# A decoder layer on one core: wide activations transposed by DMA, block maxima folded for two batches together, third norm on ScalarE, keys placed by spread DMAs, engine orders rewritten

## The chip, the cores and the metric

One core of one Trainium2 chip. The metric is the device time of one execution in microseconds. The kernel before takes 292.42 us, the median of three runs (292.4 to 292.68).

## The reference

Sixteen sequences (batches) of 128 tokens with 256 features go through one decoder layer. A post-norm follows each of three parts; the last part has a norm of its own inside.

```python
def attn(x):                     # L0_attn: q, k, v projections, no softmax
    kvt = jnp.cumsum(k * v, axis=-2) * denom
    return jnp.einsum('bse,fe->bsf', q * kvt, Wo)
def xattn(q, k, v):              # 32 query heads, 8 key heads, head size 8, 128 context rows
    weights = jax.nn.softmax(qh @ kh / sqrt(8)); return weights @ vh
def ffn(inputs):                 # blocks of 32: shared power-of-two scale, 8-bit steps
    x = residual = bf16_round(inputs)
    h = mx_layernorm(x, ln_w, ln_b)
    h = mx_gelu(mx_linear(h, W1, b1))          # 256 -> 1024
    return bf16_round(residual + mx_linear(h, W2, b2))   # 1024 -> 256
x = layernorm(x + attn(x)); x = layernorm(x + xattn(x, ctx, ctx)); x = layernorm(x + ffn(x))
```

`mx_quant`, inside `mx_linear`, takes the largest magnitude of each block of 32, cuts it to its exponent, and rounds the block's values to steps of that power of two.

## The kernel before

The 16 batches go as 8 pairs (`PB` = 2 batches, `NP` = 8). Every engine has its own hand-ordered instruction stream: a `head` written out call by call, a `step(p, on)` that is unrolled four times (t = 5 to 8), and a `tail` written out again. In step t the list `p` holds the pairs t, t-1, ... t-6, so `p[1]` is in its projections, `p[2]` and `p[3]` in cross attention, `p[4]` in the feed-forward part and `p[5]`, `p[6]` in its end. Nothing but these orders and the semaphore waits sets when work runs. A loop step thus does the work of one pair.

What the change and the prediction's steps touch:

- Cross attention. `keys_rounded` (POOL, L536 on) splits the keys into `k3r`; `keys(p, b, u)` (POOL, L555) multiplies them with a mask into the one buffer `kbd`, four instructions a pair, so that the four key heads lie on a block diagonal. PE computes the scores twice: `scores_a` (L2122) for the maxima, which DVE takes with `maxima` (L1323, 16 a pair), and `scores_b` (L2156) with the maximum subtracted, which ACT exponentiates (`exps`, L857). The maxima travel through a PE transpose (`maxT`), an ACT copy (L845) and, for the pairs 1 to 6, a small DMA issued by SP (`max_rows`, L397) into the rows of `xT`. `keys(p, ...)` waits for the last `scores_b` of the pair before, since `kbd` is single.
- The third norm. DVE's `moments` and `mean_var` of `xb_all` give mean and variance; POOL's `var_eps` (L504) and `rstd` (L509) the factor; DVE's `norm3` (L1361, two a pair) applies it; POOL's `weight3` (L593) and `shift3` (L599) apply weight and shift; DVE's `quantise_h` (seven steps: L1411, 1414, 1416, 1418, 1420, 1422, 1424) quantises both batches together.
- The wide activations `g_sb` (128 x 1024 a batch, after the gelu). `quantise_g(p, b, i)` on DVE has ten steps a batch: magnitude (L1465), two foldings by halves (L1467, 512 and 256 columns), a reduction to 32 block maxima (L1470), three steps on 32 columns (L1414, 1416, 1418), and three over 1024 columns (L1420, 1422, 1424). Then PE transposes the result (`g_T`, L2222, eight matmuls a batch), ACT copies it into `gT` (`gT_copy`, L881), and PE multiplies (`ffn_down`, L2233 and L2235).
- The end of a pair. ACT's `y2_copy` (L912), POOL's `ffn_out` (L605) and `residual3` (L612), DVE's moments, the norm on ACT (`norm4`, L903), and the store by SP.
- Weights. In the head DVE quantises both weight matrices between the other work (L1242 to L1271).
- `warm`, `warm_p` and `warm_last` on PE (L2001, L2013, L2007) are matmuls of zeros whose results nobody reads.

## Time and profile before

| what | value |
| --- | --- |
| median of the runs | 292.42 us |
| time of the profiled execution | 291.33 us |
| its span, first to last instruction | 289.6 us |
| mean granted TensorE clock | 0.988 |
| PE busy | 270.8 us (94%), 1640 matmuls |
| DVE busy | 261.2 us (90%), 682 instructions |
| ACT busy | 220.2 us (76%), 378 instructions |
| POOL busy | 174.1 us (60%), 253 instructions |
| DMA | 12.68 MB, mean 44 GB/s |

Spans of PE, DVE and ACT overlap with the next instruction's, so that a row's mean duration is longer than what the instruction takes from its engine; the distance from start to start, where nothing is waited for, is what it takes. The chain that ended last runs 44% on PE, 37% on DVE, 6% on ACT and 3% on POOL.

### The profile page before, as it was taken

How to read it: one execution, taken by the hardware profiler on the slowest of the kernel's cores; microseconds unless marked ns; L12 is line 12 of the kernel's file. 1: busy time of each engine (PE TensorE's matmuls, PEld its weight loads, DVE VectorE, ACT ScalarE, POOL GpSimd, SP SyncE). 2: the span in 40 equal slices, each digit the busy share in tenths (PEclk: the TensorE clock that was granted, in tenths of full speed). 3: DMA queues.
4: the chain of work that ended last, by engine and by line, in shares of the span. 5: the costliest groups of instructions: out<-in, count | busy, mean ns of one | idle time of the engine just before them, and what ended most of it. 6: DMA issues, size and time to landing. Idle time of an engine off the chain costs nothing.

```text
span 289.6 us, 5338 instructions
## 1 busy us (share of the span) xinstructions
PE 270.8 (94%) x1640; PEld 165.4 (57%) x1640; DVE 261.2 (90%) x682; ACT 220.2 (76%) x378; POOL 174.1 (60%) x253
## 2 busy tenths in 40 slices
PE   8999998999997998999989998999699989997799
PEld 3776755477554764676566756575346444543454
DVE  3799999996999999999999999999986997799982
ACT  5131866479999699979998889889998899875650
POOL 2746380698466787868786878667777353533321
PEclk9999999999999999999999999999869999999999
DMA  7931200002110020022002200210010000100111
GB/s 239 381 125 36 65 3 0 9 6 71 37 43 0 8 71 15 1 67 77 16 1 63 79 9 5 66 44 9 7 36 5 3 0 0 37 3 1 37 38 38
DMA packets 11053, 12.68 MB, mean 44 GB/s; under 512 B 3216, under 2 KB 8336, under 8 KB 10768
## 3 DMA queue, kind: packets, MB, share of 16 engines
q1 hardware_dynamic: 10592, 11.55, 12.5%
q10 hardware_dynamic: 432, 0.79, 0.7%
q8 instruction: 13, 0.21, 0.3%
q14 instruction: 16, 0.13, 0.2%
HBM read 9.84 MB, written 2.10 MB: 41 GB/s over the span
## 4 chain that ended last, share of the span: by engine, by line
PE 44%; DVE 37%; issue 8%; ACT 6%; POOL 3%; DMA 1%; DVEq 0%; POOLq 0%
DVE nm L1323 9%; PE bank L2122 6%; PE bank L2156 6%; PE bank L2169 5%; DVE st L1278 4%; PE bank L2007 3%; PE bank L2235 3%; PE bank L2210 3%; PE bank L2056 2%; PE bank L2082 2%; DVE gq L1424 2%; PE bank L2069 2%; PE bank L2208 2%; ACT g_sb L877 1%; PE bank L2177 1%
## 5 line engine op out<-in xcount | busy, mean ns | idle before, releaser
L1323 DVE TENSOR_REDUCE nm<-bank 128x4 f32<-128x512 f32 x128 | 83.8, 677 | 0.8 <-PE bank L2122 0.6
L857 ACT ACTIVATE p_sb<-bank 128x512 f32<-128x512 f32 x128 | 72.3, 599 | 12.1 <-PE bank L2156 11.6
L2122 PE MATMUL bank<-kbd,xT 96*128 96x512 f32 x128 | 56.0, 468 | 2.6 <-ACT xT L828 1.5
L2156 PE MATMUL bank<-xT,kbd 104*128 104x512 f32 x128 | 53.0, 444 | 5.3 <-DMA xT<-mT 3.2
L555 POOL TENSOR_TENSOR kbd<-k3r,diag_sb 96x512 fp32r<-96x512 f32 x32 | 33.2, 1052 | 12.9 <-PE bank L2156 12.9
L2156 PEld LDWEIGHTS bank<-xT,kbd 104*128 104x128 f32 x128 | 24.6, 193 | 18.6 <-ACT p_sb L857 6.4
L2122 PEld LDWEIGHTS bank<-kbd,xT 96*128 96x128 f32 x128 | 24.4, 193 | 17.9 <-DVE nm L1323 10.8
L2169 PE MATMUL bank<-p_sb,va_sb 128*32 128x512 f32 x256 | 33.3, 610 | 0.0
L509 POOL TENSOR_TENSOR rs<-ve,nhalf 128x2 f32<-128x2 f32 (+1 forms) x36 | 26.1, 725 | 4.6
L504 POOL TENSOR_SCALAR ve<-mv 128x2 f32<-128x2 f32 (+1 forms) x36 | 8.4, 234 | 33.5 <-DVE mv L1284 31.8
L2043 PE MATMUL bank<-wkv_r,xt_r 128*128 128x512 f32 x84 | 23.8, 405 | 0.7 <-DVE r_sb L1301 0.7
L871 ACT ACTIVATE y_sb<-bank 128x512 bf16<-128x512 f32 x32 | 19.1, 596 | 5.5 <-PE bank L2210 4.8
L828 ACT ACTIVATE xT<-bank 96x512 fp32r<-96x512 f32 x32 | 18.6, 586 | 5.5 <-PE bank L2106 5.4
L1278 DVE BATCH_NORM_STATS2 st<-r_sb 128x6 f32<-128x256 f32 x48 | 19.3, 416 | 0.6 <-POOL r_sb L612 0.3
L2106 PEld LDWEIGHTS bank<-idr,x 128*96 128x96 f32 x128 | 14.2, 164 | 9.5 <-issue 3.6
L2210 PE MATMUL bank<-w1T,hT 128*128 128x512 bf16 x64 | 19.1, 379 | 0.0
L2007 PE MATMUL bank<-zero_b 128*128 128x512 bf16 x80 | 18.9, 379 | 0.0
L881 ACT ACTIVATE gT<-bank 128x1024 bf16<-128x1024 bf16 x16 | 16.4, 1022 | 2.9 <-PE bank L2222 2.8
L605 POOL TENSOR_TENSOR s_sb<-y_sb,xb_all 128x512 bf16<-128x512 bf16 x7 | 8.3, 1185 | 16.7 <-ACT y_sb L912 16.7
L2043 PEld LDWEIGHTS bank<-wkv_r,xt_r 128*128 128x128 f32 x84 | 15.6, 189 | 4.5 <-issue 1.3
L2106 PE MATMUL bank<-idr,x 128*96 128x128 f32 x128 | 17.6, 261 | 0.5 <-ACT xT L850 0.5
L877 ACT ACTIVATE g_sb<-y_sb 128x1024 bf16<-128x1024 bf16 x16 | 16.9, 1057 | 0.4
(133 smaller groups left out, 619.1 us busy)
## 6 DMA issues: line engine op xcount, KB each, us to landing
xt_sb<-in_xt SPq DMA_DIRECT2D x8, 256.0 KB, 2.9
x_sb<-in_x SPq DMA_DIRECT2D x8, 256.0 KB, 2.9
out_dram<-o_sb SPq DMA_DIRECT2D x7, 256.0 KB, 2.2
k_sb<-in_ctx SPq DMA_DIRECT2D x8, 192.0 KB, 3.0
x_all<-in_w SPq DMA_DIRECT2D x1, 1024.0 KB, 6.2
w_raw<-in_w SPq DMA_DIRECT2D x1, 1024.0 KB, 8.3
p_sb<-in_wkv ACTq DMA_DIRECT2D x2, 256.0 KB, 3.9
cv_sb<-in_ctxv SPq DMA_DIRECT2D x8, 64.0 KB, 2.0
```

The costliest lines, as they stand in the source:

```text
L509: gp.tensor_tensor(rs[:, part(b)], ve[:, part(b)], nhalf[:, part(b)], ALU.pow).then_inc(rs_ready, batches(b))
L555: gp.tensor_tensor(kbd[0:MR, b, u, :, :], k3r[:, b, u, :].bitcast(F32).unsqueeze(1).to_broadcast([MR, KU, P]), diag_sb[0:MR, :].unsqueeze( ...
L857: sc.activation(p_sb[:, k, :], bankB[k % 2][:, :], ACT.Exp, scale=SCORE_SCALE).then_inc(s_ex, 1)
L1278: ve.bn_stats(st[:, b, :], rows).then_inc(st_ready, 1)
L1323: ve.tensor_reduce(nm[:, b, u, g, :], bankA[(2 + k + 11 * b) % 2][:, :].rearrange("p (k t) -> p k t", k=KU), AX.X, ALU.max, negate=True).t ...
L2007: mm(bankB[0][:, :], zero_b[:, 0:P], zero_b[:, :], start=True, stop=True)
L2043: last = mm(bankP[b][:, :], xt_r[:, a, c, b, :], wkv_r[:, w, c, :], start=c == 0 and n == 0, stop=c == KC - 1 and n == len(PARTS) - 1)
L2106: last = mm(bk[0:MR, g * P:(g + 1) * P], x3[:, b, u, g, :, :].rearrange("p a r -> p (a r)"), idr[:, :], start=True, stop=True)
L2122: mm(bankA[(2 + k + 11 * b) % 2][:, :], xT[0:MR, b, u, g, :], kbd[0:MR, b, u, :, :].rearrange("r k t -> r (k t)"), start=True, stop=True). ...
L2156: mm(bankB[k % 2][:, :], kbd[0:MR + 2 * KU, b, u, kk, :], xT[0:MR + 2 * KU, b, u, :, :].rearrange("r g s -> r (g s)"), start=True, stop=Tr ...
L2169: last = mm(value_bank(p, b)[VW * k:VW * (k + 1), :], va_sb[:, at0:at0 + VW], p_sb[:, u * KU + k, :], start=u == 0, stop=u == U - 1, tile_ ...
L2210: last = mm(bk[:, :], hT[:, c, b, :], w1T[:, c, cols], start=False, stop=c == KC - 1)
```

## The change

- `g_T` and `gT_copy` go for the pairs 0 to 4 (`BY_DMA` = 5). SP issues one transposing DMA a batch, `gT[:, b] <- gq[:, b, :]`, after the last step of `quantise_g`. `ffn_down` waits for its landing. Pairs 5 to 7 keep PE's transposes.
- `quantise_g` has six steps a batch (magnitude, foldings to 512 and 256, and the three over 1024 columns). Between them six new steps `g_scales(p, i)` work on both batches in one instruction each: foldings to 128, 64 and 32 columns a batch in place of the two reductions, and the three small steps, now on bf16 maxima. The last pair has twelve steps a batch (`last_quantise_g`) with the same foldings.
- `norm3` moves from DVE to ACT for the pairs 0 to 6 (`pair_norm3`); POOL computes its shift (`shift_product`, `shift` with `nb3`, two more small instructions a pair).
- `keys` goes from POOL for the pairs 1 to 7: SP copies the four heads by four DMAs a pair into `kbd[p % 2]`, now two buffers. Pair 0 keeps the POOL multiplications, one DMA copies the mask rows to the second buffer, and POOL zeroes it once.
- `last_x2` goes from DVE to ACT (`norm2_x2(7, b)`, behind the last gelu).
- Every head, step and tail has a new order, with other places and numbers of the `warm` matmuls.

The core of the diff:

```diff
+            def keys(p, k):
+                if k == 0:
+                    sp.wait_ge(s_k3r, 2 * p + 2)
+                    if p == 1:
+                        sp.wait_ge(s_seta, 5)
+                    else:
+                        sp.wait_ge(s_sbm, 16 * (p - 1))
+                sp.dma_start(kbd[p % 2][k:MR:KU, :, :, k, :].bitcast(F32), k3r[k:MR:KU, :, :, :].bitcast(F32)).then_inc(s_kbd, 16)
+
+            def transpose_g(p, b):
+                sp.wait_ge(s_q2[b], GSTEPS * (p + 1))
+                if later(p):
+                    sp.wait_ge(s_f2, upto(p - 1, b))
+                sp.dma_start_transpose(gT[:, b, :, :], gq[:, b, :]).then_inc(s_gTd[b], 16)
...
             def step(p, on):                         # SP
+                if on[1]:
+                    load_x(p[1])
                 if on[3]:
                     max_rows(p[3], 1)
                 if on[0]:
                     load_xt(p[0])
+                if on[2]:
+                    max_rows(p[2], 0)
                 if on[1]:
-                    load_x(p[1])
-                    load_values(p[1])
-                if on[2]:
-                    max_rows(p[2], 0)
+                    keys(p[1], 0)
+                if on[4]:
+                    transpose_g(p[4], 0)
+                if on[1]:
+                    keys(p[1], 1)
                 if on[5]:
                     store(p[5])
+                if on[1]:
+                    keys(p[1], 2)
+                    load_values(p[1])
+                    keys(p[1], 3)
+                if on[4]:
+                    transpose_g(p[4], 1)
                 if on[0]:
                     load_keys(p[0])
...
             def step(p, on):                         # POOL, from its middle
                 if on[4]:
                     var_eps(p[4], mv3, ve3, s_mv3, s_ve3)
                     rstd(p[4], ve3, rs3, s_ve3, s_rs3)
+                    shift_product(p[4], mv3, rs3, nb3, s_rs3, s_nb3)
+                    shift(p[4], nb3, s_nb3)
+                if on[2]:
+                    split_x1_high(p[2], 1)
+                if on[4]:
                     weight3(p[4])
                     shift3(p[4])
-                if on[2]:
-                    keys(p[2], 0, 0)
-                    keys(p[2], 0, 1)
+                if on[0]:
+                    split_xt_high(p[0])
                 if on[5]:
                     ffn_out(p[5])
                     residual3(p[5])
...
+            def pair_norm3(p, b):                    # ACT
+                act.wait_ge(s_nb3, 2 * p + 2)
+                sc.activation(h0_sb[:, b, :], batch_of(xb_all, p, b), ACT.Identity, bias=nb3[:, 1, b:b + 1],
+                              scale=rs3[:, b:b + 1]).then_inc(s_h0, 1)
...
+            def fold_g(batches, i):                  # DVE
+                if i == 0:
+                    return ve.tensor_scalar(gz2[:, batches, :].bitcast(U16), g_sb[:, batches, :].bitcast(U16),
+                                            MAGNITUDE, None, ALU.bitwise_and)
+                into = am2 if i == FOLDS - 1 else gz2
+                n = F >> i
+                return ve.tensor_tensor(into[:, batches, 0:n], gz2[:, batches, 0:n], gz2[:, batches, n:2 * n], ALU.max)
+            def g_scales(p, i):
+                if i == 0:
+                    for b in range(PB):
+                        dve.wait_ge(s_q2[b], GSTEPS * p + BATCH_FOLDS)
+                else:
+                    dve.wait_ge(s_gs, SSTEPS * p + i)
+                both = slice(0, PB)
+                folds = FOLDS - BATCH_FOLDS
+                last = fold_g(both, BATCH_FOLDS + i) if i < folds else scale_step(both, i - folds)
+                last.then_inc(s_gs, 1)
...
             def step(p, on):                         # DVE, its end
                 if on[4]:
+                    g_scales(p[4], 0)
                 if on[3]:
                     mean_var(p[3], 1, st2, mv2, s_st2, s_mv2)
                 if on[4]:
+                    g_scales(p[4], 1)
+                    g_scales(p[4], 2)
+                    g_scales(p[4], 3)
+                    g_scales(p[4], 4)
+                    g_scales(p[4], 5)
                 if on[0]:
                     k_times_v(p[0], 0)
+                if on[4]:
+                    quantise_g(p[4], 0, 3)
+                    quantise_g(p[4], 1, 3)
+                    quantise_g(p[4], 0, 4)
+                    quantise_g(p[4], 0, 5)
```

In the new DVE step `quantise_h(p[4], 0)` comes behind `maxima(p[2], 0, 0)`; before it came ahead of it. The new DVE step begins with `maxima(p[3], 1, 1)`, `quantise_g(p[5], 1, 4)`, `maxima(p[3], 1, 2)`, `quantise_g(p[5], 1, 5)`. In the new ACT step the two `pair_norm3` stand directly behind `q_copy`. In the new PE step `ffn_down(p[5], 0)` and `(p[5], 1)` keep their places behind `maxT(p[3], 1)` and `x1T(p[2], 0, 1)`, and `q_proj(p[1], 1)` stands eight calls earlier.

## Rows read from the trace of the kernel before

**Rows 1.** Busy time by stretch: start:end, length, then each engine's busy us (instructions)
```profile
20.00:40.00 20.00, 19.44 (x110) 13.71 (x110) 19.89 (x44) 9.64 (x18) 12.90 (x20) 1.00 0.12 37
```
**Rows 2.** The same view for one whole loop step
```profile
118.71:148.33 29.62, 28.72 (x182) 18.47 (x180) 28.54 (x76) 26.81 (x49) 22.64 (x32) 1.00 0.13 39
```
**Rows 3.** Groups by line and shape, 60 to 210 us: busy, mean ns, idle before
```profile
L1323 DVE TENSOR_REDUCE nm<-bank 128x4 f32<-128x512 f32 x82 | 53.5, 676 | 0.5 <-PE bank L2122 0.4
```
**Rows 4.** DVE timeline, end of a loop step: start, us, instruction
```profile
117.37 0.59 DVE L1470 TENSOR_REDUCE am<-gz 128x32 f32<-128x256 bf16 x1
117.87 0.17 DVE L1284 BATCH_NORM_AGGREGATE mv<-st 128x2 f32<-128x6 f32 x1
...
118.42 0.17 DVE L1416 TENSOR_SCALAR sc<-am 128x32 bf16<-128x32 f32 x1
...
118.71 0.69 DVE L1424 TENSOR_TENSOR gq<-gz,sc 128x1024 bf16<-128x1024 bf16 x1
```
**Rows 5.** DVE timeline, middle of the same step
```profile
125.64 0.73 DVE L1361 TENSOR_SCALAR h_sb<-xb_all,mv,rs 128x256 f32<-128x256 bf16 x2
126.29 1.28 DVE L1323 TENSOR_REDUCE nm<-bank 128x4 f32<-128x512 f32 x2
...
129.32 0.69 DVE L1411 TENSOR_REDUCE am<-h_sb 128x16 f32<-128x512 bf16 x1 [0.55 <-POOL h_sb L599]
...
130.35 0.96 DVE L1416 TENSOR_SCALAR sc<-am 128x16 bf16<-128x16 f32 x1
...
132.83 0.95 DVE L1424 TENSOR_TENSOR hq<-z,sc 128x512 bf16<-128x512 bf16 x1
```
**Rows 6.** POOL timeline beside rows 5
```profile
129.25 2.04 POOL L555 TENSOR_TENSOR kbd<-k3r,diag_sb 96x512 fp32r<-96x512 f32 x2
132.34 1.16 POOL L605 TENSOR_TENSOR s_sb<-y_sb,xb_all 128x512 bf16<-128x512 bf16 x1 [1.05 <-ACT y_sb L912]
```
**Rows 7.** Timelines of the head: DVE, then POOL
```profile
40.39 2.42 DVE L1268 TENSOR_SCALAR wqb<-wz 128x512 bf16<-128x512 int16 x1
...
44.85 0.49 DVE L1268 TENSOR_SCALAR wqb<-wz 128x512 bf16<-128x512 int16 x2
...
40.63 2.03 POOL L555 TENSOR_TENSOR kbd<-k3r,diag_sb 96x512 fp32r<-96x512 f32 x2
```
**Rows 8.** ACT timeline, middle of the same step
```profile
126.44 1.02 ACT L881 ACTIVATE gT<-bank 128x1024 bf16<-128x1024 bf16 x1
127.36 0.59 ACT L837 ACTIVATE q_sb<-bank 128x512 f32<-128x512 f32 x1
```
**Rows 9.** PE timeline, middle of the same step
```profile
128.54 0.27 PE L2233 MATMUL bank<-bias_h,ones_b 96*128 96x256 bf16 x1
...
130.36 0.28 PE L2233 MATMUL bank<-bias_h,ones_b 96*128 96x256 bf16 x1
```
**Rows 10.** DMA issues: count, KB each, median us to landing; then SP's timeline
```profile
xt_sb<-in_xt SPq DMA_DIRECT2D x8, 256.0 KB, 2.9
...
w_raw<-in_w SPq DMA_DIRECT2D x1, 1024.0 KB, 8.3
...
129.04 0.63 SPq L397 DMA_DIRECT2D xT<-mT  x1
```
**Rows 11.** Tail: DVE timeline, then PE timeline
```profile
219.24 0.69 DVE L1411 TENSOR_REDUCE am<-h_sb 128x16 f32<-128x512 bf16 x1 [2.87 <-POOL h_sb L599]
...
220.27 0.17 DVE L1416 TENSOR_SCALAR sc<-am 128x16 bf16<-128x16 f32 x1
220.47 0.17 DVE L1418 TENSOR_SCALAR in<-sc 128x16 int16<-128x16 int16 x1
...
221.54 0.42 DVE L1424 TENSOR_TENSOR hq<-z,sc 128x512 bf16<-128x512 bf16 x1
...
279.42 0.69 DVE L1424 TENSOR_TENSOR gq<-gz,sc 128x1024 bf16<-128x1024 bf16 x1
...
280.81 0.61 PE L2222 MATMUL bank<-idb,gq 128*128 128x128 bf16 x8
```

More of the change, by code:

```diff
@@ L33 @@
 EXPONENT = 0x7F800000
+EXPONENT16 = 0x7F80
 TINY = 2.0 ** -110
@@ L122, in decoder_kernel @@
         k3r = sb("k3r", [MR, PB, U, P], F32R)
-        kbd = sb("kbd", [P, PB, U, KU, P], F32R)
+        kbd = [sb(f"kbd{n}", [P, PB, U, KU, P], F32R) for n in range(2)]
         cv_sb = sb("cv_sb", [P, PB, KV, DH], F32)
@@ L272, in decoder_kernel @@
         s_nb2 = sem("shift2")
+        s_nb3 = sem("shift3")
         s_nb4 = sem("shift4")
@@ L290, in decoder_kernel @@
         s_q2 = [sem(f"g_quantised{b}") for b in range(PB)]
+        s_gs = sem("g_scales")
+        s_gTd = [sem(f"gT_landed{b}") for b in range(PB)]
         s_gTp = sem("g_transposed")
@@ L414, in head @@
                 load_x(0)
+                load_weight("w2")
+                load_keys(1)
+                load_xt(2)
+                load_x(1)
                 load_bias()
-                load_weight("ln")
-                load_weight("w2")
-                load_values(1)
-                load_x(1)
-                load_xt(2)
-                load_keys(1)
-                load_keys(2)
-                load_x(2)
-                load_xt(3)
+                load_xt(3)
+                load_keys(2)
+                keys(1, 0)
+                keys(1, 1)
+                load_x(2)
+                keys(1, 2)
+                keys(1, 3)
+                keys(2, 0)
+                second_diagonal()
+                load_values(1)
+                load_weight("ln")
+                max_rows(1, 0)
+                keys(2, 1)
+                keys(2, 2)
+                load_xt(4)
+                keys(2, 3)
+                max_rows(1, 1)
+                spread_bias()
                 load_values(2)
-                max_rows(1, 0)
-                max_rows(1, 1)
                 load_x(3)
                 load_keys(3)
-                spread_bias()
-                load_xt(4)
                 max_rows(2, 0)
+                keys(3, 0)
+                transpose_g(0, 0)
+                keys(3, 1)
+                load_keys(4)
+                keys(3, 2)
+                keys(3, 3)
                 load_values(3)
-                load_keys(4)
+                transpose_g(0, 1)
             def step(p, on):
+                if on[1]:
+                    load_x(p[1])
                 if on[3]:
@@ L980, in head @@
                 pv_copy(1, 0)
                 weights(2)
-                x1T(2, 0, 1)
+                q_copy(3)
                 exps(1, 1, 0)
+                weights(3)
                 exps(1, 1, 1)
-                weights(3)
                 exps(1, 1, 2)
+                hT_copy(0)
                 exps(1, 1, 3)
-                hT_copy(0)
                 exps(1, 1, 4)
+                hidden(0, 0, 0)
+                norm2_x2(0, 0)
                 exps(1, 1, 5)
-                hidden(0, 0, 0)
@@ L1694, in step @@
                     q_times_sum(p[1])
+                if on[2]:
+                    maxima(p[2], 0, 0)
                 if on[4]:
@@ L1813, in tail @@
                 quantise_h(5, 3)
+                maxima(7, 0, 0)
                 quantise_h(5, 4)
@@ L2392, in head @@
+                scores_a(2, 0, 0)
                 weights_T(2)
-                x1T(2, 0, 1)
+                scores_a(2, 0, 1)
+                running_sum(3)
+                scores_b(1, 1, 0)
+                weights_T(3)
+                scores_b(1, 1, 1)
+                values_back(1, 0)
+                scores_a(2, 0, 2)
+                scores_a(2, 0, 3)
+                scores_b(1, 1, 2)
+                h_T(0)
+                scores_b(1, 1, 3)
+                scores_a(2, 0, 4)
+                scores_b(1, 1, 4)
@@ L2431, in step @@
                 if on[3]:
+                    scores_a(p[3], 1, 0)
+                if on[1]:
+                    kv_proj(p[1], 0, 1)
+                if on[3]:
+                    x1T(p[3], 1, 1)
                     scores_b(p[3], 0, 0)
@@ L2474, in step @@
                     ffn_down(p[5], 0)
+                if on[2]:
+                    x1T(p[2], 0, 1)
+                    scores_a(p[2], 0, 0)
+                if on[5]:
+                    ffn_down(p[5], 1)
                 if on[3]:
@@ L2477, in step @@
                 if on[2]:
-                    x1T(p[2], 0, 1)
-                if on[5]:
-                    ffn_down(p[5], 1)
-                if on[2]:
-                    scores_a(p[2], 0, 0)
+                    scores_a(p[2], 0, 1)
                 if on[3]:
@@ L2554, in tail @@
                 weigh(6, 0, 0)
+                x1T(7, 0, 0)
                 maxT(6, 1)
-                g_T(4, 1)
-                x1T(7, 0, 0)
+                weigh(6, 0, 1)
+                scores_a(7, 0, 0)
                 x1T(7, 0, 1)
-                weigh(6, 0, 1)
+                warm_p(2)
                 ffn_down(4, 0)
+                scores_a(7, 0, 1)
                 scores_b(6, 1, 0)
```

1181 lines of the change are left out of this document (579 added, 602 removed).

## The prediction, as made before the run

> **What bounds the kernel now.** I read busy time by stretch first. In the head DVE is busy 19.89 of 20 us while ACT has 9.64 and POOL 12.90 [rows 1]. Then one whole loop step: 29.62 us, DVE 28.54, PE 28.72, ACT 26.81, POOL 22.64 [rows 2]. Two engines look full, so the groups decide: the 82 maxima that DVE takes between 60 and 210 us, each of which needs a fresh PE result, waited 0.5 us for PE in all [rows 3]. PE keeps ahead of DVE, its spans overlap, and its many short matmuls stretch when it has time. DVE is the bound from 20 us to about 210 us. There I count DVE time from start to start, and ask of each edit what it takes from DVE, and whether DVE will find its next input ready. The last 80 us are a chain from engine to engine in which DVE sometimes waits, as at 219.24 for POOL's h, 2.87 us [rows 11].
>
> **The change part by part.** The sum is made against the profiled execution (291.33 us, span 289.6); the median of the runs is 1.1 us above it, and I carry the difference over to the median.
>
> 1. *The third norm leaves DVE.* Two instructions, from 125.64 to the next start at 126.29: 0.65 us a pair [rows 5]. For the pairs 0 to 4 this lies where DVE is full: 5 x 0.65 = -3.25. For pairs 5 and 6 DVE waits for POOL anyway [rows 11], so nothing.
>
> 2. *Block maxima for two batches.* Out go, a pair, two reductions of 0.50 from start to start [rows 4] and six small steps, of which two took 0.29 from 118.42 to 118.71, 0.15 each: 1.0 + 0.9 = 1.9. In come six instructions that wait for one another. A dependent small step takes 0.20 from start to start (220.27 to 220.47) [rows 11]; three make 0.60, and the three foldings, which have 256, 128 and 64 results, lie between that 0.20 and the 0.50 of the reduction over 256 inputs: I take 0.35, 0.27 and 0.23. Together 1.45. That gains 0.45, but the new order also puts steps that wait for each other side by side (the last two over 1024 columns of batch 0, and the high and low part of the maxima), where the filler between them had hidden a delay of 0.1 to 0.2 each: about 0.35 back, and the gain that remains I take as 0. Bounds: -0.8 a pair if the foldings overlap with other work, +0.5 if they don't and each costs a reduction's 0.50.
>
> 3. *POOL in DVE's way.* The scale step of `quantise_h` on 16 columns took 0.96 us at 130.35, while POOL ran two `keys` from 129.25 to 131.29 [rows 5, 6]; without a neighbour the same step took 0.17 [rows 11]. This stands in four pairs (the scale step of the pairs 1 to 4, one in each of four loop-long periods), with 0.1 more on the step in front of it each time: 4 x 0.89 = -3.56. Behind it the last step of `quantise_h` took 0.95 beside POOL's `ffn_out` [rows 5, 6] against 0.42 alone [rows 11]; whether they still meet depends on the new order, so I take half, 4 x 0.27 = -1.06 (bounds 0 and -2.1). In the head a step of the weights took 2.42 us at 40.39 beside two `keys` [rows 7]; two of its size took 0.49 together at 44.85, and nothing idles there: -2.1. The POOL instruction now behind `shift3` is `split_xt_high`, 0.62 us long, which ends within the 0.69 us reduction ahead of the scale step; should it start late it would cost up to 0.6 a pair. The Trainium skill, page SBUF — State Buffer, section Who interferes with whom, says that a DVE instruction in a mode with two ports and a GpSimd instruction exclude one another for the whole length of the one that was first; by that, `split_xt_high` would hold the scale step as `keys` did, if it comes a microsecond late, and the sum would be 2.4 us poorer. The trace agrees with the exclusion itself (0.96 against 0.17).
>
> 4. *The longer way to h.* POOL now computes a product and a shift (0.25 each) before ACT may norm. ACT reaches the place behind `q_copy`, which started at 127.36, 0.59 us long [rows 8]. ACT has lost two copies in front of it (1.02 each, 0.91 from start to start) and got one norm of 0.5 there, so `q_copy` ends near 126.6; two norms to 127.7; `weight3` and `shift3` 2.65, to 130.35. Now h was ready at 129.29, where DVE had waited 0.55 [rows 5]. DVE arrives 0.65 earlier without `norm3` and 0.6 later with one of the maxima put ahead. So it waits 1.7 us in place of 0.55 in the worst case, +1.15, and in the best case, with ACT earlier by the scores that PE now delivers sooner, no more than today. I take +0.8, nearer to the end that is worked out, for the four loop steps: +3.2 (bounds 0 and +7.4, the latter if it waits 1.85 more).
>
> 5. *Transposes by DMA.* They take 16 transposes a pair from PE (eight in 0.61 at 280.81 [rows 11]) and two copies from ACT. Neither is the bound: 0 to the sum. The price is in the landing. Batch 0's last step ends at 119.40 [rows 4], and `ffn_down` starts at 128.54 and 130.36 [rows 9]: 9.1 us for the first; the second batch's last step comes about 3 us into the step, which leaves 7.9. A plain load of 256 KB lands in 2.9 us, and one of 1 MB in 8.3 [rows 10]. I take a landing near the first row, hidden: 0. Behind the transposes in SP's queue stand `load_keys`, `load_x` and `max_rows`; the small DMA of the maxima is issued at 129.04 with 0.63 us on the queue [rows 10], about 5 us after the second transpose can go. At 0.4 to 0.6 us for each issue that is enough.
>
> 6. *Keys by DMA.* POOL loses 4 x 1.04 us a pair; four more issues on SP, each a copy of under 64 KB, have nearly a whole step until `scores_a` needs them: 0. In the head POOL stood behind PE before the `keys` of pair 1, since `kbd` was single, with the first norm of pair 2 queued behind; DVE was full with weights then [rows 1], so 0 as well, with up to -1.5 in reserve.
>
> 7. *The end.* `last_x2` off DVE, twelve steps for ten in the last pair (+0.2), and four instead of six zero matmuls ahead of the last `g_T`, which started at 280.81 behind them though its input, begun at 279.42, had been ready at 280.11 [rows 11]. Gain 0.7 to 0.9, less 0.2: -0.7.
>
> Sum: -3.25 + 0 - 3.56 - 1.06 - 2.1 + 3.2 - 0.7 = -7.5. That makes 283.8 for an execution like the profiled one, and 292.4 - 7.5 = 284.9 us for the median.
>
> **The rivals.**
>
> - *The wait for h takes the gain.* Were h ready 2.35 us later than taken against DVE's arrival in each of four steps, +9.4 would stand in place of +3.2: 291.1 us. For it speaks that h already ends last in every step (0.55) and 2.87 us in the tail [rows 5, 11]; against it, that ACT gets freer just there. 0.12.
> - *The transposes land late: slower.* Mechanism: both wait in one queue, one after the other, and PE stands in front of `ffn_down` with all scores behind it. It decides from a duration of about 5.5 us each (two of them against the 11 us from 119.40 to 130.36). At the 8.3 us that a plain 1 MB takes [rows 10], batch 1 lands near 136.0, 5.6 us late, five pairs: +28, so 313 us. For it: the trace has no transposing DMA at all, and such a transfer may be cut into far smaller pieces than a load. Against: 16 DMA queues are idle in the loop for 87% of the time [rows 2]. 0.12. The Trainium skill speaks on both sides: VectorE: DVE Perf Modes, section The three transpose paths, gives 1309 ns for one 128 x 128 bf16 block by DMA, and eight of these in a row are an estimated 10.5 us, with which the total would be near 335; Advanced Engine Details and Errata, section X-Bar Transpose, calls them as fast as regular DMAs, which is the case taken above. No run here shows either yet.
> - *The new order misfits.* Head and tail are new, and POOL's and SP's waits can fall on the chain in places that I can't see: +8 to +11 against the sum, 293 to 296. 0.07.
> - *DVE overlaps better than taken* (foldings hidden, no wait for h, no `ffn_out` in the way): under 277.5 us. 0.05.
>
> **How the numbers follow.** The forecast of 284.9 us with its bounds (278 to 290) has 0.64. The range 277.5 to 294 takes in the wait for h and part of the misfit. About 0.2% is what a measurement can tell from no change. Faster by more: 0.64 + 0.05 + most of the first rival, 0.78. Within 0.2%: 0.04. Slower: 0.12 + 0.06 = 0.18.
>
> **What the profile after would show.** A loop step of 28.0 to 28.7 us (29.62 now); no L1361-like instruction on DVE in the loop; the 16-column scale step at 0.17 to 0.2; idle time of DVE before the reduction of h between 0.6 and 1.9 a step; PE never waiting for a `gT` landing, and landings under 5.5 us; DVE busy over 95% of the loop still. I am wrong if PE's wait before `ffn_down` names a DMA, if DVE's idle before h passes 2.5 us, or if the gain stands in the tail rather than in the loop.

## The result, and the profile after

The changed kernel takes 295.3 us (median of nine runs, 295.03 to 298.56), the kernel before, measured beside it, 292.42 us. The ratio, taken over all runs, is 1.0126, 95% interval 1.0093 to 1.0159: slower by some 3.7 us (2.7 to 4.6; the two medians are 2.9 us apart). I had forecast 284.9 us, 277.5 to 294.0, with 0.78 on faster.

The engines' busy time fell as forecast, the time did not. The page of the changed kernel, its busy line and its clock line:

```profile
PE 268.5 (92%) x1560; PEld 161.3 (55%) x1560; DVE 252.7 (86%) x656; ACT 219.0 (75%) x384; POOL 150.2 (51%) x242
...
PEclk9997999999999999999999999999999999999999
```

DVE lost 8.5 us of busy time, POOL 23.9 us. Busy time of the changed kernel over one whole loop step (columns as in [rows 1]; answers [rows 2]):

```profile
149.70:179.30 29.60, 28.38 (x166) 17.85 (x165) 26.35 (x72) 25.95 (x48) 18.56 (x30) 1.00 0.30 63
```

The step is still 29.6 us long (three steps on the mean: 29.74 us, before 29.69), and DVE now stands idle over 3 us of it. What it waits for, in the groups by line and shape, 60 to 210 us (answers [rows 3]):

```profile
L1391 DVE TENSOR_REDUCE nm<-bank 128x4 f32<-128x512 f32 x81 | 53.7, 679 | 10.9 <-PE bank L2213 10.6
```

The maxima waited 0.5 us for PE in before and 10.9 us now: what DVE saved in the loop, it spends waiting for PE. PE isn't full either: in the same three steps it is busy 27.7 us a step (28.4 in before). The weight loads of its score tiles wait for DVE's maxima to free a bank, 11.2 us in 24 waits between 118 and 238 us (4.1 us in 8 waits in before), so the two engines wait for each other. The single steps behaved as forecast. DVE timeline, middle of a loop step of the changed kernel (answers [rows 5]):

```profile
162.90 0.69 DVE L1391 TENSOR_REDUCE nm<-bank 128x4 f32<-128x512 f32 x1 [1.42 <-PE bank L2213]
163.86 0.69 DVE L1474 TENSOR_REDUCE am<-h_sb 128x16 f32<-128x512 bf16 x1 [0.27 <-POOL h_sb L656]
...
164.79 0.17 DVE L1479 TENSOR_SCALAR sc<-am 128x16 bf16<-128x16 f32 x1
...
166.53 0.43 DVE L1487 TENSOR_TENSOR hq<-z,sc 128x512 bf16<-128x512 bf16 x1
```

The scale step is at 0.17 (0.96), hq's last step at 0.43 (0.95), and h is waited for 0.27 us (0.55). The transposing DMAs, in the list of DMA issues (median us to landing), then SP's timeline:

```profile
gT<-gq SPq DMA_TRANSPOSE x10, 3.1
...
153.91 1.26 SPq L428 DMA_TRANSPOSE gT<-gq  x1
```

They land in 3.1 us and PE never waits for one. So the loop gave nothing back; what was lost stands mostly at the two ends. Start times from the four traces that matter, in us from the first instruction (and the span):

| event | before | changed | a_diag0 | a_head2 |
| --- | --- | --- | --- | --- |
| first exponential of pair 0 | 33.1 | 36.7 | 33.2 | 34.7 |
| first exponential of pair 3 | 117.2 | 119.3 | 117.0 | 117.3 |
| first exponential, batch 1 of pair 7 | 244.7 | 246.0 | 243.9 | 244.7 |
| last gelu | 274.6 | 278.8 | 276.7 | 277.5 |
| span, to the last instruction | 289.6 | 293.4 | 291.3 | 292.0 |

Read down the changed kernel's column: 3.6 us late after the head, of which 1.3 are left at batch 1 of pair 7; 2.9 us lost from there to the last gelu; 0.4 gained behind it. That is the 3.8 us by which this trace is longer. A trace is one execution: that of a_head2 is the longest of its twelve runs, and the others have spans of 289.8 to 291.8 us, so differences of 1 us between traces count for little, and the shares of head and tail don't add up to the microsecond.

### The profile page after: what moved, and what is told of

The parts are those of the page before. It is cut to its first block and busy times, and to the rows that moved or that the text cites. A ratio compares the mean times of both kernels' runs of the same rounds, so it can differ in the third digit from the quotient of the medians.

```text
span 293.4 us, 5216 instructions
## 1 busy us (share of the span) xinstructions
PE 268.5 (92%) x1560; PEld 161.3 (55%) x1560; DVE 252.7 (86%) x656; ACT 219.0 (75%) x384; POOL 150.2 (51%) x242
## 5 line engine op out<-in xcount | busy, mean ns | idle before, releaser
L2213 PE MATMUL bank<-kbd,xT 96*128 96x512 f32 x128 | 60.4, 479 | 6.8 <-ACT xT L883 3.9
L2262 PE MATMUL bank<-p_sb,va_sb 128*32 128x512 f32 x256 | 32.8, 602 | 2.2 <-ACT p_sb L912 2.2
L561 POOL TENSOR_SCALAR ve<-mv 128x2 f32<-128x2 f32 (+1 forms) x36 | 7.5, 208 | 49.6 <-DVE mv L1352 48.4
L2249 PEld LDWEIGHTS bank<-xT,kbd 104*128 104x128 f32 x128 | 23.8, 189 | 13.5 <-ACT p_sb L912 7.2
L888 ACT ACTIVATE v_sb<-bank 128x256 f32<-128x256 f32 x16 | 6.1, 382 | 22.7 <-PE bank L2131 20.0
L2095 PE MATMUL bank<-zero_b 128*128 128x512 bf16 x80 | 20.0, 379 | 0.0
L2170 PE MATMUL bank<-wo_sb,vh_sb 128*128 128x256 f32 x64 | 17.4, 398 | 2.2 <-DVE vh_sb L1362 2.2
L641 POOL TENSOR_TENSOR r_sb<-x_all,att 128x512 f32<-128x512 f32 x7 | 9.0, 1285 | 19.5 <-DVE att L1418 13.9
```

Source lines behind the costliest of these rows:

```text
L2095: mm(bankB[0][:, :], zero_b[:, 0:P], zero_b[:, :], start=True, stop=True)
L2213: mm(bankA[(2 + k + 11 * b) % 2][:, :], xT[0:MR, b, u, g, :], kbd[p % 2][0:MR, b, u, :, :].rearrange("r k t -> r (k t)"), start=True, stop ...
L2249: mm(bankB[k % 2][:, :], kbd[p % 2][0:MR + 2 * KU, b, u, kk, :], xT[0:MR + 2 * KU, b, u, :, :].rearrange("r g s -> r (g s)"), start=True, ...
L2262: last = mm(value_bank(p, b)[VW * k:VW * (k + 1), :], va_sb[:, at0:at0 + VW], p_sb[:, u * KU + k, :], start=u == 0, stop=u == U - 1, tile_ ...
```

## Experiments: the head

DVE timeline of the changed kernel, 19 to 24 us, then PE's and POOL's of the same time, then two stretches of busy time:

```profile
19.25 1.19 DVE L1374 TENSOR_SCALAR x_all<-r_sb,mv,rs 128x256 f32<-128x256 f32 x1
20.48 2.13 DVE L1286 CAST kbd<-diag_sb 32x512 fp32r<-32x512 f32 x2
22.63 0.59 DVE L1380 TENSOR_SCALAR x<-x_all 128x256 fp32r<-128x256 f32 x1
23.15 0.67 DVE L1362 TENSOR_TENSOR vh_sb<-bank,q_sb 128x512 f32<-128x512 f32 x1
...
23.87 1.97 PE L2170 MATMUL bank<-wo_sb,vh_sb 128*128 128x256 f32 x4 [2.19 <-DVE vh_sb L1362]
...
19.26 1.04 POOL L612 TENSOR_TENSOR kbd<-k3r,diag_sb 96x512 fp32r<-96x512 f32 x1
...
21.00 1.32 POOL L588 TENSOR_TENSOR xt_r<-xt_sb,xt_r 128x512 fp32r<-128x512 f32 x1
...
21.00:25.00 4.00, 1.81 (x7) 1.06 (x6) 3.97 (x7) 0.00 (x0) 3.61 (x5) 0.88 0.22 70
25.00:29.00 4.00, 4.00 (x14) 2.49 (x13) 2.81 (x5) 0.00 (x0) 0.87 (x3) 0.70 0.27 74
```

The norm (L1374), 0.4 us elsewhere, takes 1.19, the two halves of the diagonal rows 2.13 together (0.76 for the same two at 35.63, beside only small steps of POOL). Behind them stands the product that `out_proj(1)` needs, so PE stands still for 2.19 us, and after it the granted clock is 0.70 on the mean of 25 to 29 us. This is the exclusion that step 3 of the prediction counted as a gain; the new order of the head put it where it hurts.

**a_diag0**, the changed kernel with

```diff
 first_low(0)
+diagonal_rows(0)
 first_low(1)
...
 first_norm1(1)
-diagonal_rows(0)
 first_x1_high(1)
```

> The changed kernel with one line moved: the diagonal rows of the first pair are laid again right behind VectorE's first subtraction (about 5.6 us), where the kernel before has them, and no longer at 20.5 us beside GpSimd's key and split work, where they took 2.13 us. Theory 'head' (the head's new order costs the changed kernel 3 us or more, by VectorE standing in GpSimd's way just ahead of the values' product that out_proj(1) waits for): 2 to 3.5 us less than the changed kernel, so 292 to 293.3 us, with the wait of 2.19 us before out_proj(1) gone or under 0.5 us. Rival 'absorbed' (another engine's queue sets the step later, so an early start is lost again): within 0.7 us of 295.3 us, with the exponentials of the later pairs at the same times as in the changed kernel.

Measured 1.0063 [1.0041, 1.0085] against the kernel before, so 1.8 us less than the changed kernel. (Here and below every ratio is against the kernel before, run in the same session; two variants are compared by their ratios.) PE and the clock in the same place:

```profile
21.86 1.13 PE L2170 MATMUL bank<-wo_sb,vh_sb 128*128 128x256 f32 x4
...
25.00:29.00 4.00, 3.74 (x14) 2.12 (x13) 3.97 (x10) 0.69 (x2) 0.80 (x3) 1.00 0.49 136
```

The wait of 2.19 us is gone and the clock stays at 1.00. **a_head2** moves the product ahead as well:

```diff
-first_norm1(1)
-first_x1_high(1)
 q_times_sum(1)
 maxima(0, 0, 0)
+first_norm1(1)
 maxima(0, 0, 1)
+first_x1_high(1)
```

> As a_diag0, and the values' product of pair 1 and the first maximum are put ahead of the second batch's first normalisation, as in the kernel before. Theory 'head': another 1 us or so, 291 to 292.5 us, and no dip of the granted clock at 22 to 29 us, since TensorE no longer stands still there. Rival 'absorbed': 295 us. A third way: the second batch's x1 comes later and its scores wait for it; then it is slower than a_diag0 by up to 1 us.

Measured 1.0033 [1.0011, 1.0054]. By the ratios that is 0.9 us less again, but the two intervals overlap and the trace doesn't show it, so the second step isn't told from nothing. Both together are clear: the places of three calls in the head are 2.7 of the 3.7 us by the ratios, give or take over 1 us. The wait and the fall of the clock went together in a_diag0, so what each of them cost is not told apart.

## Experiments: the parts in the kernel before

Each part alone, with the order of the kernel before kept as far as the part allows, and all four together. (The move of `last_x2` was not tried by itself.)

> The kernel before with one part: keys of pairs 1 to 7 spread by four DMAs each into two key tiles, GpSimd's 28 products (1.0 us each) left out. The prediction's step 3: 0.89 us a step from the scale step, 0.5 us from hq and 2.1 us in the head, 285.5 to 289 us. Theory 'VectorE does not set the step': the contention goes but VectorE only waits longer, so the head's part alone is left, 290 to 292.5 us. Rival 'queue': SyncE's 28 issues of 0.8 us delay the loads behind them, 293 us or more.

**b_keys** 0.998 [0.995, 1.001]: the same. In the trace the scale step takes 0.17 at 129.45, and the weight step that took 2.42 us [rows 7] takes 0.35 at 40.27: the first exponential of pair 1 comes 1.8 us earlier (58.5 for 60.3 us). At pair 3 it is 0.9 us ahead and by batch 1 of pair 7 0.2 us (244.5 for 244.7), and the mean step is 29.67 us. The stall was real and its removal worth nothing in the loop. The trace also shows that DVE was not let go earlier: the last step of `quantise_h`, 0.95 us in before, now meets more of POOL's `ffn_out` and takes 1.39 us in all four steps, and 0.35 us go into a wait for PE. From the reduction of h to the maximum behind `hq` it is 4.37 us in b_keys and 4.38 in before.

> The kernel before with one part: g of pairs 0 to 4 turned by DMA (3 to 4 us from issue to landing in the changed kernel), TensorE's 80 transposes and ScalarE's ten copies of 1.03 us left out. The prediction's step 5: 0, so 292 us. Theory 'TensorE sets the step': up to 1.2 us a pair less, 286 to 290 us. Rival 'transposes land late': TensorE waits ahead of ffn_down, 293 us or more.

**b_gdma** 1.001 [0.998, 1.004]: the same, mean step 29.64. Put together, the two are not their sum:

> The kernel before with two parts together, keys by DMA and g turned by DMA. Each alone left the time and the step of 29.6 us as they were (0.998 and 1.001), though the first takes 4 us of work off GpSimd's step and the stalls of VectorE with it, and the second 1 us off TensorE's. Theory 'two bounds of one size' (VectorE's own row and TensorE's own row each fill 29.6 us, so taking from one shows nothing): the two together give 0.4 to 0.9 us a step, 286.5 to 289.5 us. Rival 'a loop over several engines' that neither shortens: within 0.3% of 292.2 us.

**b_kg** 1.021 [1.018, 1.024]. Neither expectation had it; the mean step is 31.45 us. PE's waits, 118 to 236 us (us in total, times, longest), then SP's timeline:

```profile
PE bank L2273 <- DMA gT<-gq: 5.2, 6, 1.4
...
155.25 0.40 SPq L425 DMA_DIRECT2D out_dram<-o_sb  x1
155.69 1.65 SPq L415 DMA_DIRECT2D kbd<-k3r  x2
157.44 1.28 SPq L421 DMA_TRANSPOSE gT<-gq  x1
158.77 0.57 SPq L371 DMA_DIRECT2D k_sb<-in_ctx  x1
159.47 1.24 SPq L421 DMA_TRANSPOSE gT<-gq  x1
```

g of the first batch was ready at 150.69 us, its transposition was issued at 157.44, behind the store, which waits for its data, and two key copies of 0.8 us each. I had put the transposes at the end of SP's step; the changed kernel puts them ahead, and there nobody waits. I read it as the queue's place and not the landing; no run moved the transposes inside b_kg. (In b_gdma, with the same place and no key copies, the first batch's went out 5.0 us after its data, and nobody waited.)

> The kernel before with one part: the last folds and the scale steps of g for both batches at once, in the places of the old steps. The prediction's step 2: -0.8 to +0.5 us a pair, taken as 0, so 288.5 to 294.5 us, likeliest 292. Theory 'TensorE sets the step': no change, 291.5 to 293 us. Rival 'g is finished later' (the first batch's product now waits for the second's folds, so g's transposes stand in TensorE's queue): 293 to 298 us, with TensorE waiting for gq.

**b_folds** 1.041 [1.038, 1.044]: the step grows to 31.4 us. The first batch's last step now waits for the second batch's foldings, and PE stands at its transposes; its timeline:

```profile
154.75 0.62 PE L2266 MATMUL bank<-idb,gq 128*128 128x128 bf16 x8 [1.32 <-DVE gq L1479]
```

> The kernel before with one part: the third norm of pairs 0 to 6 on ScalarE, with its shift worked out on GpSimd, all else in place. The prediction's theory (step 1): 0.65 us less a pair over five steps, so 289.2 us, less what the longer way to h costs (up to 0.8 us a step, then 292.4 us). Theory 'TensorE sets the step': within 0.7 us of 292.4 us. Rival 'h is waited for': 293 to 296 us, with VectorE idle before the block maxima of h by over 1.4 us (0.55 us in before).

In short (places of the calls as comments):

```diff
 exps(p[3], 0, 7)
...
-norm3(p[4], b)                 # DVE, ahead of maxima(p[3], 1, 6); both batches
+pair_norm3(p[4], b)            # ACT, behind gT_copy(p[5], 1) and q_copy(p[1])
+shift_product, shift of nb3    # POOL, behind rstd of ve3
```

**b_norm3** 1.108 [1.105, 1.111], 31 us: by far the dearest part, and no theory of mine had more than 4 us on it. DVE waited 27.1 us for h. I tried the two obvious mends,

> As b_norm3, which stood 10.8% over the kernel before with VectorE waiting 27.1 us for h in seven waits. Two places differ: ScalarE norms right behind the last exponential of the first batch (before g's copy and q's copy, 1.5 us earlier), and VectorE takes the next pair's first maximum before it waits for h, as the changed kernel does. Theory 'VectorE stands at h and holds back the maxima that TensorE needs' : most of the 31 us goes, 293 to 299 us. Rival 'the norm on ScalarE costs by itself' (its 1.1 us and the exponentials behind it): over 305 us. The prediction's steps 1 and 4 would give 289 to 293 us.

**b_norm3b** 1.105 [1.100, 1.109], no better, and then took the keys out of POOL's queue, since they stood behind h in the chain of waits:

> b_norm3b (third norm on ScalarE, 1.10 of the kernel before) with the keys spread by DMAs as well. In b_norm3b the chain of waits of a step runs from ScalarE's norm over GpSimd's weighting of h (171.2 us) to the two key products queued behind it (173.9 us) and to TensorE's scores (176.0 us). Theory 'interlock' (the late h costs so much only because the next pair's keys stand behind it in GpSimd's queue): with the keys off GpSimd most of the 30 us goes, 291 to 297 us. Rival 'h itself is on the path' (the up-projection or VectorE waits for h): above 305 us. The prediction's sum for these two parts (steps 1, 3, 4) would be 289 us.

**b_norm3k** 1.104 [1.101, 1.108]. The theory of the interlock falls. Its trace shows where the time goes: DVE's timeline, then POOL's, then PE's, then a stretch of busy time:

```profile
172.70 0.69 DVE L1364 TENSOR_REDUCE nm<-bank 128x4 f32<-128x512 f32 x1 [2.10 <-PE bank L2156]
...
174.69 1.04 DVE L1459 TENSOR_SCALAR in<-sc 128x16 int16<-128x16 int16 x1
175.76 0.80 DVE L1461 TENSOR_TENSOR z<-h_sb,in 128x512 int16<-128x512 bf16 x1
176.59 1.24 DVE L1463 TENSOR_SCALAR z<-z 128x512 bf16<-128x512 int16 x1
177.93 0.64 DVE L1465 TENSOR_TENSOR hq<-z,sc 128x512 bf16<-128x512 bf16 x1
...
174.54 1.15 POOL L649 TENSOR_TENSOR r_sb<-x_all,s_sb 128x512 f32<-128x512 f32 x1
175.66 0.62 POOL L563 TENSOR_SCALAR xt_r<-xt_sb 128x512 fp32r<-128x512 f32 x1
176.37 1.31 POOL L568 TENSOR_TENSOR xt_r<-xt_sb,xt_r 128x512 fp32r<-128x512 f32 x1
...
178.63 0.61 PE L2228 MATMUL bank<-idb,hq 128*128 128x128 bf16 x4 [3.93 <-DVE hq L1465]
...
179.00:185.00 6.00, 6.00 (x18) 3.47 (x16) 4.57 (x12) 3.48 (x6) 0.70 (x1) 0.54 0.00 0
```

h was ready at 171.2 us, but DVE stood at the maximum that I had put ahead of it until 172.7; so its steps for h met POOL's residual and splits and took 1.04, 0.80, 1.24 and 0.64 where the changed kernel has 0.17, 0.42, 0.28 and 0.43 (2.4 us more). PE stood 3.93 us at `h_T` with the scores queued behind it, and for the next six microseconds the granted clock was 0.54, near the lower of its two levels (1.2 GHz), where each score tile takes 0.43 us for 0.23: an estimated 3 us more (6 us at 0.54). The wait and the clock together are about the 6 us by which this step is longer (35.5 on the mean of three for 29.7). That is a reading of one trace; no run mended the wait at `h_T`. In the changed kernel the order of PE and DVE around h is another, and h is waited for 0.27 us.

> The kernel before in its own order, with all four parts of the change and none of its reordering: third norm on ScalarE, keys by spread DMAs with two key tiles, block maxima folded for both batches, g turned by DMA for five pairs. The prediction's theory (VectorE sets the step, so each part's saving on it counts): 284 to 287 us. Theory 'TensorE sets the step' (it is 97% busy in a step of before, and what VectorE saves turns into waiting for TensorE): the only part that frees TensorE is the eight transposes per batch (1.2 us of busy time a pair, five pairs), so 286 to 291 us at best, and 290 to 293 us if that time is not on TensorE's path. If the new order were needed for the parts to pay, 292 to 296 us.

**b_all** 1.133 [1.128, 1.138]. It has b_norm3's place for the norm, so it says only that the parts don't pay in this order.

## Experiments: what holds the step

The chain of waits of the kernel before runs through one step like this (start, us, what; only its turns are shown):

```profile
118.71 0.69 DVE gq L1424
...
122.13 0.50 PE bank L2122
...
137.49 0.20 PE bank L2082
137.70 0.51 DVE nm L1323
...
142.38 0.25 PE bank L2134
...
143.37 0.61 ACT y_sb L871
144.00 1.07 ACT g_sb L877
...
145.09 0.43 DVE gz L1465
...
148.33 0.69 DVE gq L1424
```

DVE has it from 118.7 to 122.1, PE alone from 122.1 to 137.7, DVE again to 142.3, PE and ACT's gelu to 145.1, and DVE to the end of the step. Four of my terms lie in PE's stretch: `norm3`, the scale step, hq and the wait for h. I tested that with work left out on either side.

**b_hshort**: `quantise_h` on 128 of 512 columns. **b_gshort**: in `quantise_g` the magnitude, the scaling and the minimum on 256 of 1024 columns, the scaling by a constant in place of the blocks' factors.

> The kernel before with part of its work left out: h's quantisation is made on a quarter of the columns, so its output differs. That takes some 1.5 to 2 us a pair from VectorE (hq and the scale step that stood 0.96 us each among it) in the stretch of the step where the chain of waits of before runs over TensorE alone (122 to 137.7 us). Theory 'VectorE sets the step': 1.5 to 2 us a step, 280 to 285 us. Theory 'a loop over several engines, this stretch beside it': within 0.3% of 292.2 us. Theory 'two bounds': at most 0.9 us a step, as b_gshort, 287 to 290 us.

> The kernel before with part of its work left out: of g's quantisation, the magnitude, the scaling and the minimum are made on a quarter of the columns, so its output differs. That takes some 2 us a pair from VectorE just where the chain of waits of before runs over VectorE (144 to 149.6 us of the step that starts at 118.7). Theory 'two bounds' (TensorE's row is next at 28.7 us busy): at most 0.9 us a step, 287 to 290 us. Theory 'VectorE sets the step' (the prediction's): 2 us a step, 278 to 283 us. Theory 'a loop over several engines, this stretch in it': also 278 to 284 us, and b_hshort gains much less.

**b_hshort** 1.001 [0.999, 1.003], **b_gshort** 0.985 [0.983, 0.988]. One whole step of each, busy time, b_hshort first:

```profile
146.60:176.20 29.60, 28.55 (x182) 18.54 (x181) 28.44 (x76) 26.65 (x48) 22.63 (x32) 1.00 0.14 39
...
147.00:175.70 28.70, 28.03 (x181) 18.41 (x180) 26.80 (x76) 26.34 (x48) 21.97 (x32) 1.00 0.13 40
```

b_hshort is a weaker test than I meant it to be, for DVE's busy time hardly fell (28.44 for 28.54 us). DVE's timeline, in the second of the four loop steps, then in the fourth:

```profile
132.29 1.06 DVE L1425 TENSOR_TENSOR hq<-z,sc 128x128 bf16<-128x128 bf16 x1
...
191.46 0.21 DVE L1425 TENSOR_TENSOR hq<-z,sc 128x128 bf16<-128x128 bf16 x1
192.60 0.69 DVE L1324 TENSOR_REDUCE nm<-bank 128x4 f32<-128x512 f32 x1 [0.94 <-PE bank L2124]
```

In the first three steps the shorter instructions stood behind POOL's for as long as the long ones had (a quarter of hq's columns took 1.06 us), so nothing was saved. In the fourth hq took 0.21 us, and DVE then waited 0.94 us for PE: the next maximum starts 4.35 us after the reduction of h, as in the others. So in this stretch time off DVE is worth nothing, and that rests on one step. Less work where the chain runs over DVE, 1.7 us of busy time a step, is worth 0.6 us a step (29.07 on the mean of three for 29.69), and more at the end: of the 4.2 us by which the trace is shorter 2.3 fall behind batch 1 of pair 7.

For TensorE I left out work in the same way. **b_pelight** is the kernel before, and **b_gsp** is b_gshort, each without the bias products of the feed-forward layers (`mm(bk, ones_b, bias_h[:, cols], start=True, stop=False)` and its like):

> The kernel before with the bias products of both feed-forward layers left out on TensorE, so its output differs. By the chain of waits they take 0.23 us each in the first layer and 0.12 us in the second, 1.2 us a pair, all in TensorE's stretch of the chain. b_gsp showed that the same edit gives 1.0% on top of b_gshort. Theory 'the loop binds, TensorE's stretch 15.6 us of it': up to 1.2 us a step less, 286 to 289 us. Theory 'VectorE's own row of 29.1 us is the first bound and TensorE's the second': within 0.3% of 292.2 us.

> b_gshort (g's magnitude, scaling and minimum on a quarter of the columns, 0.985 of before, step 28.7 to 28.8 us) with the bias products of both feed-forward layers left out on TensorE too, 2.2 us of its busy time a pair. Theory 'TensorE's row is the next bound at 28.7 us': the step falls on, to 26.7 to 28 us, and the time to 274 to 283 us. Rival 'the next bound is VectorE's or a loop without TensorE': within 0.3% of b_gshort, 286.5 to 288 us.

**b_pelight** 1.000 [0.998, 1.003], **b_gsp** 0.976 [0.973, 0.978]. The four corners: 1.000 with both full, 1.000 with PE lighter, 0.985 with DVE's g lighter, 0.976 with both. PE's saving shows only when DVE's is there. b_pelight is a warning about the chain too: its 1.2 us a step lie in PE's stretch of it, and gave nothing. I take it that two rows run side by side between 122 and 138 us, equally long; both shortened at once was not tried.

In the changed kernel it is the other way round. **a_gshort** and **a_pelight** make the same two edits on a_head2 (1.0033):

> a_head2 (the changed kernel with its head mended, 1.003 of before) with the same part of g's quantisation left out as in b_gshort, 2 us of VectorE's work a pair. Theory 'the changed kernel's step of 29.6 us is set by the loop over g's scales' (after the joint folds VectorE does four wide steps in a row at 151.5 to 155.3 us while the next maxima wait, although it stands idle 3.2 us elsewhere in the step): 1 us a step or more, 284 to 288 us. Rival 'TensorE's row or the score loop sets it': within 0.3% of a_head2, 291.5 to 293 us.

> a_head2 with the same bias products left out, so its output differs. Taking 2 us a pair off VectorE's quantisation of g in this kernel left its step at 29.5 us (a_gshort). Theory 'TensorE with its waits for the score banks sets the changed kernel's step': 1.2 us a step less, 285 to 288 us. Rival 'the loop of scores, maxima and exponentials sets it whatever else TensorE does': within 0.3% of a_head2, 291.5 to 293.5 us.

**a_gshort** 1.007 [1.004, 1.010], not better than a_head2. **a_pelight** 0.995 [0.993, 0.997], 2.5 us under a_head2. The latter is less than TensorE's row alone would give (285 to 288 us expected, 290.7 by the ratio). So TensorE with its waits holds much of the changed kernel's step and DVE's work there lies beside it; what holds the rest, the exchange of banks between the two or something else, stays open.

**c_order** tried to use the chain: b_keys with the incoming pair's residual and moments behind the maxima and their halves, and g's first step ahead.

The calls, shortened:

```diff
-residual1(p[1])
 maxima(p[2], 0, 6), maxima(p[2], 0, 7)
-moments(p[1], 0), moments(p[1], 1)
 quantise_g(p[4], 0, 0)
 max_high(p[2], 0) ... max_low(p[2], 0)
+residual1(p[1]), quantise_g(p[4], 0, 2), moments(p[1], 0), moments(p[1], 1)
```

> b_keys with four lines of VectorE's step reordered: the residual and the moments of the pair coming in (1.3 us) are made behind the maxima and their halves, no longer ahead of them, where the chain of waits of before runs over VectorE (137.7 to 142.3 us) into TensorE's transposition of the maxima. Theory 'a loop over several engines with TensorE's row at 28.7 us right behind': 0.3 to 0.9 us a step, 286 to 290 us. Rival 'VectorE's own row sets the step' (the order of its work makes no difference): within 0.3% of b_keys' 0.998.

**c_order** 1.009 [1.006, 1.011], step 30.4: a loss where the chain had promised 0.3 to 0.9 us a step. The chain ran elsewhere at once. DVE's timeline:

```profile
140.38 0.43 DVE L1482 TENSOR_SCALAR gz<-g_sb 128x1024 uint16<-128x1024 uint16 x1 [0.61 <-ACT g_sb L894]
```

The work that I moved back had covered ACT's gelu (1.28 us of table load and 1.07 of work); without it DVE waits for g.

## Experiment: the tail

From batch 1's first exponential of pair 7 to the last gelu it is 29.9 us in before and 32.8 us in the changed kernel, in a_diag0 and in a_head2: 2.9 us that have nothing to do with the head. In a_head2 h of pair 6 came at 250.2 us, 247.7 in before. **a_tail6** gives pair 6's norm back to DVE:

> a_head2 with the third norm of pair 6 back on VectorE, behind the first scaling of g of pair 5, and its shift gone from GpSimd. In a_head2 h of pair 6 was ready at 250.2 us against 247.7 us in before, and its last quantising step ended 2.8 us later. Theory 'longer way to h is paid in the tail' : 1 to 2 us less than a_head2, so 0.997 to 1.000 of the kernel before. Rival 'the tail is set by g of pair 5 and the chain of pair 7': within 0.3 us of a_head2's 1.003.

Measured 1.010 [1.007, 1.012], 1.8 us worse than a_head2. DVE's, POOL's and PE's timeline:

```profile
245.35 1.64 DVE L1533 TENSOR_TENSOR gq<-gz,sc 128x1024 bf16<-128x1024 bf16 x1
246.91 1.49 DVE L1532 TENSOR_SCALAR gz<-gz 128x1024 bf16<-128x1024 int16 x1
...
244.53 1.92 POOL L650 TENSOR_TENSOR h_sb<-h_sb,lnwb_sb 128x512 f32<-128x512 f32 x1 [0.75 <-DVE h_sb L1425]
246.59 1.53 POOL L656 TENSOR_TENSOR h_sb<-h_sb,lnwb_sb 128x512 bf16<-128x512 f32 x1
...
247.05 0.62 PE L2313 MATMUL bank<-idb,gq 128*128 128x128 bf16 x8 [1.35 <-DVE gq L1533]
```

h came at 248.1, as wanted, but POOL's two steps for it fell beside g's last steps on DVE: 1.64 us for 0.69 and 1.49 for 0.42, and PE waited for gq. The late h in the tail is thus seen, its price isn't: the mend brought stalls of its own. Which of the tail's lines hold the 2.9 us stays open.

A further difference stands where the loop ends. Busy time and clock of before, then of the changed kernel:

```profile
207.90:214.70 6.80, 6.24 (x26) 3.35 (x25) 6.78 (x15) 6.38 (x13) 5.22 (x8) 0.50 0.10 33
...
209.60:213.60 4.00, 3.10 (x12) 1.40 (x12) 3.76 (x10) 3.68 (x8) 1.80 (x6) 1.00 0.00 0
```

Before ran these 6.8 us at the lower level and the changed kernel did not, and still the time from the first exponential of pair 6 to that of pair 7 is 29.4 us in before and 30.3 in the changed kernel, where PE waits 2.53 us for ACT's copy of `xT` at 207.1 and 1.14 us for a maximum at 212.7. No run tests these two waits. Of all kernels that do the whole work none beat the kernel before; b_keys and b_gdma are level with it.

## Why the prediction was wrong, step by step

- *What bounds the kernel.* Here it failed. I read "the maxima hardly wait for PE" [rows 3] as "DVE is the bound", and then counted every microsecond on DVE between 20 and 210 us in full. That view says that DVE finds its input ready; it doesn't say how far off the next bound is. PE was busy 28.72 of 29.62 us in the same step [rows 2], and the chain of waits, which I hadn't printed by the microsecond, has PE alone for half of it. The runs show it: in the changed kernel DVE has 2.2 us less to do a step, the step is as long as before, and DVE's maxima wait 10.9 us for PE; taking more from DVE there gives nothing (a_gshort), taking from PE does (a_pelight, 2.5 us). In the kernel before 1.7 us off DVE are worth 0.6 a step (b_gshort). DVE was one bound of before, but the other stood within 0.6 us of it. What hung on this in the sum are step 1 and the loop's share of step 3, together -7.9 us, and it came to about nothing.
- *Step 1, norm3, -3.25.* DVE lost the work; it lay in PE's stretch of the chain, and no gain is seen in the loop. Alone in the old order it cost 31 us.
- *Step 2, foldings, 0.* Right for DVE's time: the six joint steps take 1.35 us (179.43 to 180.78), 1.45 forecast. Unseen was who waits for batch 0, now later: 1.7 us a step in the old order (b_folds); in the new one PE has no transposes of it to wait with.
- *Step 3, POOL in DVE's way, -6.7.* In the changed kernel every size came as forecast (0.17 for 0.96, 0.43 for 0.95, and in b_keys 0.35 for 2.42), and it was worth nothing in the loop; in b_keys' head 1.8 us came, and 0.2 were left at pair 7. The same exclusion, put by the new order in front of `out_proj(1)`, is the first part of the loss. I had asked where it goes, not where it comes.
- *Step 4, the way to h, +3.2.* h was waited for 0.27 us, below my lower end. In the tail, where I had set it at nothing, h came 2.5 us later (a_head2 against before); what that cost is not shown.
- *Step 5, transposes, 0.* Right: 3.1 us to landing, hidden, and the rival at 313 falls. The Trainium skill gives 1309 ns for one block of 128 x 128 (VectorE: DVE Perf Modes, The three transpose paths); my estimate of 10.5 us for eight in a row doesn't hold, since all eight landed in 3.1 us. By another page of the Trainium skill (Advanced Engine Details and Errata, X-Bar Transpose) they are as fast as regular DMAs, and the trace agrees: a plain load of the same 256 KB landed in 2.9 us. b_kg points to SP's queue as the risk.
- *Step 6, keys, 0.* Right (b_keys).
- *Step 7, the end, -0.7.* About right where it was made: from the last gelu to the end it is 14.6 us for 15.0. The 2.9 us are lost ahead of the last gelu, in the new order of the tail, for which the sum had no term.
- *The rivals.* "The new order misfits", 293 to 296 us, with 0.07, has the right number, in part by luck: it set 8 to 11 us of misfit against a gain of 7.5, and there were some 3 to 4 against a gain of about nothing. Its mechanism is seen in the head, where DVE stood behind POOL. A schedule written anew for five engines deserved far more than 0.07, since I could see none of its waits. None of the three signs of being wrong that I had named came; the one that did, DVE's maxima waiting for PE, wasn't among them, though DVE at 89% of the loop step, not over 95%, said the same.

## What to carry to other kernels

Where an unrolled loop has several full engines, take the chain of waits through one whole step before costing anything, and don't count an edit where the chain doesn't run over its engine. Where it does, the chain still gives no more than an upper bound (b_pelight 0 for 1.2 us a step, c_order a loss): ask which row is next, for here one stood a few tenths behind. The cheap test is to leave work out, in two places and on two engines, alone and together; then look in the trace whether the time was taken off at all, since a shorter DVE step that stands behind POOL is no shorter (b_hshort). A part that moves work to another engine can't be costed apart from the order around it: alone, the four parts here cost nothing (keys, transposes), 4.1% (foldings) and 10.8% (norm), and the two that cost nothing alone cost 2.1% as a pair.

## What the runs showed of the hardware

- A pause of TensorE can be paid twice. In b_norm3k five waits of 3.7 to 4.2 us before `h_T` all came with the lower level of the clock, for 3.4 or 6.8 us each; a score tile of 0.23 us took 0.43. The length of a single wait below that doesn't decide it: after 2.19 us the changed kernel fell to the lower level for 3.4 us, after 2.53 us (209.6) it kept 1.00, and before, after 1.19 us (206.95), had 0.50 for 6.8 us. (PE was busy 2.76 of the 4.9 us ahead of that fall, and 1.94 of the 4.6 us ahead of 209.6, where there was none.)
- The exclusion of DVE and POOL reaches small steps most: 16-column steps of 0.17 took 0.96 and 1.04, a step of 0.42 took 1.49, and a step cut to a quarter of its columns took 1.06 where it needs 0.21. So work taken off such a step can save nothing. The maxima, which read a bank of TensorE's results, kept their 0.6 us from start to start beside POOL (23.74 us in the changed kernel, two in 1.27, while POOL rounded keys). The Trainium skill (SBUF — State Buffer, Who interferes with whom) agrees on the exclusion.
- A transposing DMA of 128 x 1024 bf16 holds SP's queue for 1.26 us and lands in 3.1; a copy of keys, 48 KB, holds it 0.8 us.
